# Routed experts, last stage: the eight row scatters of the last octet, one at every third tile instead of eight in a row

## The reference

```python
x = x + tanh(g_xattn[0]) * L0_xattn(ctx, layernorm(x), mask, ...)
x = x + tanh(g_ffn[0])   * L0_ffn(layernorm(x), ...)      # 16 soft experts
x = x + tanh(g_xattn[1]) * L1_xattn(ctx, layernorm(x), ...)
x = x + tanh(g_ffn[1])   * L1_ffn(layernorm(x), ...)      # 8 routed experts
```

```python
logits = xf @ router_w.T
routing = softmax(logits); top_w, top_i = top_k(routing, 2)
top_w = top_w / sum(top_w)
g = einsum('nd,ehd->neh', xf, w_gate); u = einsum('nd,ehd->neh', xf, w_up)
y = einsum('neh,edh->ned', silu(g) * u, w_down)
out = einsum('ned,ne->nd', y, combine)
```

## Time and profile before

| | us |
|---|---|
| median of 3 timed runs | 1481.29 |
| lowest, highest | 1478.18, 1482.33 |
| span of the profiled execution | 1498.2 |
| PE busy in it | 1377.6 (92%) |
| POOL busy in it | 523.2 (35%) |
| the expert stage in it, first load to the end | about 1310 to 1498 |

### The profile page before, as it was taken

One profiled execution on the slowest core, in us unless ns is written; L12 is line 12 of the kernel. 1 busy time (PEld: TensorE's weight loads), 2 busy tenths in 40 slices (PEclk: granted clock), 3 DMA queues, 4 the chain that ended last, 5 costly groups with the idle time before them and its releaser, 6 DMA issues. The chain is left out here.

```text
span 1498.2 us, 33716 instructions
## 1 busy us (share of the span) xinstructions
PE 1377.6 (92%) x12029; PEld 1171.5 (78%) x12029; DVE 953.4 (64%) x2374; ACT 1012.3 (68%) x2019; POOL 523.2 (35%) x510
## 2 busy tenths in 40 slices
PE   5898699899999999999999999988999999876985
PEld 4887588788888888888888888877778888755773
DVE  6998767666766767667667666552455555654455
ACT  5887487577677676776776767647788888633552
POOL 3112355322322322323223223302235555635553
PEclk9999899999999999999999999999999999998998
DMA  8300100399940000000000000022000000022236
GB/s 221 88 1 1 58 2 1 77 176 102 102 30 2 2 1 2 2 2 2 2 2 1 2 1 2 1 73 57 1 29 14 17 16 16 30 69 63 76 97 174
DMA packets 124980, 60.46 MB, mean 40 GB/s; under 512 B 41945, under 2 KB 120241, under 8 KB 124690
## 3 DMA queue, kind: packets, MB, share of 16 engines
q1 hardware_dynamic: 120274, 48.92, 18.2%
q0 software_dynamic: 4544, 9.38, 1.9%
HBM read 28.84 MB, written 29.44 MB: 39 GB/s over the span
## 5 line engine op out<-in xcount | busy, mean ns | idle before, releaser
L1349 DVE SCALAR_TENSOR_TENSOR hidden<-psU,b_cols,gelu 128x512 f32<-128x512 f32 x256 | 191.4, 750 | 170.1 <-ACT gelu L1474 104.9
L1474 ACT ACTIVATE gelu<-psG,b_cols 128x512 f32<-128x512 f32 x256 | 176.2, 689 | 109.6 <-PE psG L142 96.2
L1296 POOL TENSOR_TENSOR combine_sum<-combine_sum,combineT 128x512 f32<-128x512 f32 x48 | 63.3, 1319 | 294.9 <-ACT combineT L1488 294.9
L1325 POOL TENSOR_TENSOR dispatchT<-dispatchT,dispatch_inv 128x512 f32<-128x512 f32 x64 | 67.7, 1057 | 232.6 <-DVE dispatch_inv L1453 232.6
L1608 PE MATMUL psU<-w_down,hidden 128*64 128x128 f32 x2048 | 123.4, 273 | 0.0
L1608 PE MATMUL psDown<-w_down,hidden 128*64 128x128 f32 x2048 | 122.7, 273 | 0.0
L1861 POOL TENSOR_TENSOR probs<-probs,row_sum 128x512 f32<-128x512 f32 x64 | 66.2, 1035 | 143.6 <-DVE row_sum L1974 142.6
L1608 PEld LDWEIGHTS psU<-w_down,hidden 128*64 128x64 f32 x2048 | 113.2, 137 | 1.3 <-issue 1.2
L1608 PEld LDWEIGHTS psDown<-w_down,hidden 128*64 128x64 f32 x2048 | 113.9, 137 | 0.1
L140 PE MATMUL psG<-slots_hi,w_gate_hi 128*128 128x512 f32 x256 | 105.9, 414 | 1.1 <-ACT gelu L1474 0.6
L2038 ACT ACTIVATE probs<-psS,neg_max 128x128 f32<-128x128 f32 x256 | 91.2, 384 | 22.8 <-DVE neg_max L1971 18.4
(11 more groups left out here) (406 smaller groups left out, 3617.6 us busy)
## 6 DMA issues: line engine op xcount, KB each, us to landing
sorted_x<-empty_rows SPq DMA_DIRECT2D x1, 12736.0 KB, 77.5
tile_rows<-sorted_x SPq DMA_DIRECT2D x78, 65.0 KB
sorted_x<-empty_rows SPq DMA_DIRECT2D x1, 4544.0 KB, 29.9
expert_ys<-expert_y SPq DMA_DIRECT2D x16, 256.0 KB, 3.7
x<-in_x SPq DMA_DIRECT2D x8, 256.0 KB, 5.9
ctx<-in_ctx SPq DMA_DIRECT2D x8, 256.0 KB, 5.9
w_gate_raw<-in_L_ffn_Wg SPq DMA_DIRECT2D x1, 2048.0 KB, 10.9
w_up_raw<-in_L_ffn_Wu SPq DMA_DIRECT2D x1, 2048.0 KB, 16.1
```

The lines of the kernel that those rows point to most:

```text
L1325: pool.tensor_tensor(e[:], e[:], over(rb[:], SEQ, 2), ALU.mult).then_inc(s["eb_normed"], 1)
L1349: dve.scalar_tensor_tensor(hid[e][:, half, :], U[half][:], bcol[:, 1, 4 * ch + 2 * e + half:][:, 0:1], gel[half][:], ALU.add, ALU.mult).th ...
L1474: act.activation(gel[half][:], G[half][:], ACT.Gelu, bias=bcol[:, 0, 4 * ch + 2 * e + half:][:, 0:1]).then_inc(s["gelu"], 1)
```

## The change

Octet 7's eight scatters are no longer issued one after another ahead of the store of tile 16. One is issued ahead of the store of each of the tiles 16, 19, 22, 25, 28, 31, 34 and 37, and behind each POOL waits on `scattered[1]` until that scatter has landed (16 more for each).

```diff
     ADDS = N + 3 - 2 * len(GROUPS[0])
+    SCATTERS = range(16, 16 + 3 * 2 * OP, 3)
...
             for n in range(N):
-                if n == 16:
-                    for m in range(2 * OP):
-                        R.pool_scatter(pool, LAST, m)
+                if n in SCATTERS:
+                    R.pool_scatter(pool, LAST, SCATTERS.index(n))
+                    pool.wait_ge(R.scattered[LAST % RB], 16 * (2 * OP * (LAST // RB) + SCATTERS.index(n) + 1))
                 store_tile(n)
```

## The result

| | before | after |
|---|---|---|
| median | 1481.36 us | 1487.65 us |
| lowest, highest | 1478.18, 1482.33 | 1486.56, 1490.94 |
| executions | 4 | 4 |
| ratio | | 1.005 (95%: 1.0037 to 1.0062) |

By the medians the change makes the kernel 6.3 us slower, 0.42%. The ratio, to which the interval belongs, is 1.005 and stands for 7.4 us (it is not taken from the two medians). The forecast was 1485.5 us, +0.29%, with 1466 to 1490 as its range.

The account below looks back on a forecast made before the run. TensorE, busy 92%, was taken to set the pace. Against the timed median: 1481.3 + 0 for the stall + 4.3 for VectorE's wait = 1485.6 us, +0.29% (likeliest 1485.5), range 1466 to 1490.

Parts of the forecast that it names:

- Is the stall in the timed runs: TensorE's 14.7 us stall in the last stage, about 1367 to 1382 us, taken as somewhat likelier the profiled execution's own.
- Rival 1: The last stage's stall is real in every run and made by the burst: 1471 us (1466 to 1474); chance 0.38.
- Rival 3: The last stage's stall stays in either world, with POOL still issuing nearly without pause: 1481.5 us, no change; chance 0.07.
- What the eight waits hold POOL: At each octet 7 scatter: 2.50 us landing plus 0.76 us waking, 3.26 us instead of 1.26, 16 us more over eight.
- Who waits: VectorE, before writing a quad's addresses, waits for stores four quads back: 3.8 us already at quad 12, then quad 13.
- Its sum: VectorE's wait for stores by quad 13: 5.7 us, less 1.40 us of its idle time, cost 4.3 us.
- SP's wait: Ahead of quad 14, for the eighth scatter, landed by 1418.0: 9 us left for four loads, so it costs nothing.
- Rival 2: POOL falls behind much more, scatters landing after 3.0 us, VectorE's wait 10.1 us in sum: 1490 us; chance 0.10.
- The forecast's own range: The likeliest case alone, from 2.5 - 1.4 to what 2.65 us for landing would give: 1482 to 1488 us.

Follow-up runs that it names:

- run 1: The kernel before, unchanged, profiled again: 1482.41 us, ratio 0.9999.
- run 12: The kernel before with six quads of result and address buffers instead of four, repeated on another chip: 1478.87 us, ratio 1.0002.
- run 2: The change with its eight waits for landing left out, scatters still at tiles 16, 19 ... 37: 1482.71 us, ratio 0.9996.
- run 3: The change with six quads of result and address buffers instead of four: 1489.24 us, ratio 1.0039.
- run 4: The change with a wait behind every second scatter only (16, 22, 28, 34): 1482.99 us, ratio 0.9999.
- run 6: The kernel before, its burst at tile 16 kept, with a wait for landing behind each of the eight scatters: 1491.39 us, ratio 1.0077.
- run 7: The kernel before with three quads of result and address buffers instead of four, no new wait: 1485.96 us, ratio 1.0044.
- run 9: The kernel before with six quads of result and address buffers instead of four, nothing else: 1479.72 us, ratio 0.9989.
- run 11: The change with scatters four tiles sooner (12, 15 ... 33), four quads of buffers: 1484.29 us, ratio 1.0018.

## Why the prediction was right, point by point

**Is the stall in the timed runs: no, as chosen.** This choice carried the sign, and it was close to a bet: by its own chances a faster kernel (0.38) stood ahead of a slower one (0.33). The 99 executions of the kernel before, and the profile of run 1, don't have it. What it was stays open. The Trainium skill (NOTIFIC — the notification-queue block, section 7.1, Overflow) was given as a reason for laying it to the recorder. No run shows that rule at work, and one thing speaks against a general effect of recording: in runs 1 to 12 the profiled execution is never the longest of its kernel. In the change it was, with 1490.94 us against 1488.03 of the next. Rival 1, which rested on a real stall, is refuted by run 2: taking the burst apart without waits gains nothing. Rival 3, a stall that stays, falls too: no profile after the first shows it.

**What the eight waits hold POOL: 3.26 us forecast, 3.09 measured.** The mean hides that both parts were wrong. Four of eight scatters let POOL go on after 2.54 to 2.94 us, the others after 3.24 to 4.23 us. Run 3's chain has both parts: the last scatter lands after 2.30 us, not 2.50, and POOL's next store starts at 1419.56, 0.27 us behind the landing, not 0.76. The 0.76 us I had read behind a result of VectorE, not behind a landing. The slow scatters made up for both.

The Trainium skill's estimate of 2.15 us for the DMA alone (DMA: Bandwidth & Descriptors, Anatomy of one DMA — SWDGE (gpsimd) path) lies just under the 2.30 us of that landing and under every one of the eight holds; the measured times decide. The trace agrees only in part with what it puts on completion: 0.96 us of a scatter is the issuing instruction, and in run 3 another 1.34 us go by behind it until the landing.

**Who waits: VectorE, ahead of a quad's addresses, as forecast.** Casts wait near the forecast places (late in the run of scatters and behind it), the largest at 3.72 us. By the eighth scatter the stores stood 18 us behind their results, where some 16 were forecast. Runs 3, 4, 6 and 7 move this wait in both directions, and the last two come near its reckoned size: 12.1 us against 13, and 5.6 against 5.9.

**Its sum: 5.7 us forecast, 8.8 measured, the mis-sized term.** I gave POOL too much room. VectorE was to want quad 13's addresses 51.8 us after the first scatter starts (1418.1 - 1366.26); in run 1 it casts them after 49.1 (1418.52 - 1369.40). I had taken the room from the profile with the stall. Behind it the tiles were slower, 34.2 us from tile 27's scaling to tile 47's against 32.4 in run 1, and 14.7 us was too little to take off. POOL was some 0.7 us sooner than reckoned, so the cast came 7.7 us late instead of 5.7.

The other 1.1 us are waits made twice. I reckoned with a TensorE shifted by every earlier wait in full and took off VectorE's idle time once, 1.4 us. It swallows part of a wait every time: 1.1 and 1.2 us of the two long ones and the two short ones whole, 4.2 of the 8.8 us. What did not shift TensorE was waited for again at the next quad. The errors nearly cancel, 4.3 us forecast at TensorE and 4.6 measured, and that agreement is luck.

**The clock was left out.** The profiled execution loses 8.3 us from quad 6 to quad 19, and 8.3 - 4.6 = 3.7 us remain beyond TensorE's idle time. In the four stretches with a clock under 1.00, 4 x (0.24 + 0.19 + 0.10 + 0.32) = 3.4 us of full clock are missing, part of them in the idle time itself. So the clock is most of the rest there. The other three executions were 2.9 to 4.4 us shorter, and how their loss divides was not seen. The sum had no term for the clock at all, and this is the likely reason why the median came out 2 us above the forecast and clear of the 0.3% on whose edge it stood.

**SP's wait: "costs nothing" was right for the change and wrong as reckoned.** I gave it 9 us for four loads. In run 3 some 6.1 us go by from the landing of the last scatter, at 1419.3, to the turning of quad 14. The 9 us would have held that, but they contained the 5.7 us by which VectorE's wait was to delay TensorE; without that delay under 4 are left, and 2.5 were there, since TensorE stood idle for the last 3.6. A margin that exists only because another wait comes first is no cover, and run 3 lost nearly the whole 6 us there.

**Rival 2**, the larger lag, has the mechanism that was found, and its 1490 us is 2 us off on the other side: 7.7 us of lateness lie midway between the forecast's 5.7 and its 10.1. The forecast's own range was given as 1482 to 1488, but its terms add up to 1481.3 + 4.3 + 1.4 = 1487.0 at the most, and 1487.65 lies just above that: the clock, which has no term in it. The stated range of 1466 to 1490 is so wide because it had to hold both rivals.

## What to carry to other kernels

An engine that is idle for two thirds of a span can still be the slow one for 50 us. Reckon its lag against the first consumer that waits for it with finite buffers, and then against the next consumer behind that, without counting on the first to delay things. A wait for landing behind each small indirect DMA held the issuing engine 2.54 to 4.23 us here instead of 1.26, and buys nothing where nobody needs the order. Take the room from a trace that runs like the timed executions, not from one with a stall subtracted. And when the profiled span lies above every timed run, look for one stall of just that size before building on it: profile the kernel a second time.

## What the runs showed of the hardware that I had not expected

- An execution in which TensorE's results reached their consumers 2.8 to 4.2 us late, one after another, for 15 us. It came once, in the first profile, and not in 99 timed executions, the longest of 1486.53 us, nor in the profiles of runs 1, 7, 9 and 12, which have the burst too. Its cause is open.
- The landing of a scatter of 128 rows varies. Until POOL went on behind it, 2.54 to 2.59 us passed in three of the eight cases of the change, 2.94 to 3.33 in four, 4.23 in one. In run 6 it was 2.54 to 2.57 in six of eight, 3.46 and 4.06 in the others. The slow ones don't go with SP's loads: the ones of 3.29 and 3.24 us fell where none was issued.
- TensorE's clock: pauses of 2.6 and 2.0 us in the change were followed by stretches at a mean of 0.81 and 0.68 with the engine busy for all 4 us, and in run 3 a pause of 3.6 us by 4 us at 0.57. In run 11, with pauses of 1.8, 1.2 and 0.8 us, the stretches stayed at 1.00.
